# Graph network with two rounds of message passing: the matmuls of the rounds on four column strips of 32 in place of two of 64

## The reference

```python
h = jnp.maximum(_layernorm(x, axis=-1), 0.0)
for t in range(2):
    src = x[row]
    dest = x[col]
    m_input = jnp.concatenate([dest, src, edge_attr], axis=1)
    messages = m_input @ msg_W[t].T + msg_b[t]
    agg = jax.ops.segment_sum(messages, row, num_segments=x.shape[0])
    x = _gru_cell(agg, x, gru_Wih[t], gru_bih[t], gru_Whh[t], gru_bhh[t])
return x_in + x
```

## Time and profile before

| | |
|---|---|
| median of the runs | 2364.18 us (2 runs, 2361.75 to 2366.62) |
| span of the profiled execution | 2356.6 us |
| PE matmul busy | 1597.8 us (68%), 46870 records |
| PE weight loads busy | 1496.5 us (64%), 46870 records |
| DVE busy | 2175.2 us (92%) |
| ACT busy | 1953.9 us (83%) |
| POOL busy | 658.3 us (28%) |

### The profile page before, as it was taken

How to read it: one execution, slowest core, us unless ns; L and a number is a source line. 1 busy time by engine, 2 the same in 40 slices (tenths; PEclk the granted TensorE clock), 3 DMA queues, 4 the chain that set the end, 5 groups by cost and what they waited for, 6 DMA issues and landing times. The chain is left out here.

```text
span 2356.6 us, 126105 instructions
## 1 busy us (share of the span) xinstructions
PE 1597.8 (68%) x46870; PEld 1496.5 (64%) x46870; DVE 2175.2 (92%) x3629; ACT 1953.9 (83%) x4429; POOL 658.3 (28%) x853
## 2 busy tenths in 40 slices
PE   0000000000148899999999999959999999999996
PEld 0000000000138899999999999948899999999996
DVE  7999999999279899999999999958899999999996
ACT  4777895563248899999999999959899999999996
POOL 1000000000553444454544444511222222222222
PEclk9999999999959999999999999979999999999998
DMA  6100001211436666666677766647677777777773
GB/s 124 25 0 0 0 0 31 50 23 23 116 93 210 209 227 226 228 227 230 226 232 226 228 224 226 221 144 227 218 246 249 245 248 248 247 245 246 250 247 122
DMA packets 176134, 400.90 MB, mean 170 GB/s; under 512 B 73499, under 2 KB 77505, under 8 KB 175571
## 3 DMA queue, kind: packets, MB, share of 16 engines
q1 hardware_dynamic: 117047, 202.53, 27.1%
q0 software_dynamic: 57296, 195.19, 25.1%
q10 hardware_dynamic: 1708, 2.10, 0.3%
HBM read 384.73 MB, written 14.67 MB: 169 GB/s over the span
## 5 line engine op out<-in xcount | busy, mean ns | idle before, releaser
L1286 ACT ACTIVATE rows<-ps_rows 128x512 f16<-128x512 f32 x2744 | 1436.3, 647 | 47.2 <-PE ps_rows L1187 36.0
L1397 DVE TENSOR_TENSOR src<-iota_units,src_lane 128x2048 f16<-128x2048 f16 (+1 forms) x784 | 861.6, 1099 | 17.2 <-PE ps_sum L1205 13.7
L1207 PE MATMUL ps_sum<-rows,src 128*64 128x132 f16 x10976 | 585.6, 223 | 20.7 <-ACT rows L1286 14.0
L1187 PE MATMUL ps_rows<-rows_next,planes 128*64 128x128 f16 x10976 | 551.0, 220 | 32.9 <-DVE planes L1387 23.2
L1187 PE MATMUL ps_rows<-rows_now,planes 128*64 128x128 f16 x10976 | 559.8, 219 | 17.8 <-DVE planes L1387 7.8
L1205 PE MATMUL ps_sum<-src,rows 128*64 128x128 f16 x10976 | 563.9, 221 | 7.5 <-issue 6.4
L1387 DVE TENSOR_SCALAR planes<-planes,lane_no 128x2048 f16<-128x2048 f16 (+1 forms) x784 | 532.2, 679 | 5.6 <-DMA planes<-lanes_dram 5.3
L1187 PEld LDWEIGHTS ps_rows<-rows_now,planes 128*64 128x64 f16 x10976 | 425.2, 110 | 38.4 <-ACT rows L1286 14.4
L1187 PEld LDWEIGHTS ps_rows<-rows_next,planes 128*64 128x64 f16 x10976 | 412.3, 110 | 56.8 <-DVE planes L1387 23.9
L890 PE MATMUL ps_src<-ident,late 112*64 112x112 f32 x98 | 21.2, 394 | 607.3 <-DVE late L962 586.9
L1207 PEld LDWEIGHTS ps_sum<-rows,src 128*64 128x64 f16 x10976 | 404.8, 110 | 34.4 <-ACT rows L1286 21.5
(11 more groups left out here) (203 smaller groups left out, 2044.0 us busy)
## 6 DMA issues: line engine op xcount, KB each, us to landing
planes<-lanes_dram POOLq DMA_DIRECT2D x294, 512.0 KB, 4.8
planes<-lanes_dram SPq DMA_DIRECT2D x291, 512.0 KB, 4.6
planes<-lanes_dram POOLq DMA_DIRECT2D x98, 256.0 KB, 4.1
planes<-lanes_dram SPq DMA_DIRECT2D x97, 256.0 KB, 3.9
rows_now<-parts_dram SPq DMA_DIRECT2D x112, 32.0 KB, 1.7
rows_next<-parts_dram SPq DMA_DIRECT2D x112, 32.0 KB, 4.0
parts_dram<-rows_now SPq DMA_DIRECT2D x1, 3136.0 KB, 16.2
sorted_dram<-planes SPq DMA_DIRECT2D x1, 3136.0 KB, 11.6
```

The lines of the kernel that those rows point to most:

```text
L1187: last = nc.tensor.matmul(ps_rows[(u + NU * b) % 4][half * SLOTS:(half + 1) * SLOTS, k * 2 * H:(k + 1) * 2 * H], dst1[q][:, (c - q * QC) * ...
L1207: last = nc.tensor.matmul(ps_sum[b][at, 0:width], hot[:, at], row, start=(j == 0), stop=(j == J - 1))
L1286: nc.scalar.activation(rows[:, (u + NU * b) % ring, 0:n, 0:2 * H], cut(ps_rows[(u + NU * b) % 4][:])[:, 0:n, :], ACT.Copy).then_inc(rows_r ...
L1397: nc.vector.tensor_tensor(src1[q][:, 0:pairs_now], iota_units[:].rearrange("p (o l) k -> p o l k", o=1) .broadcast_to([P, pairs_now, P, 2] ...
```

## The change

All matmuls of the rounds now write 32 partitions in place of 64, and so use 32 columns of the array each; there are twice as many of them. The moving operands keep their width. The turns go through a helper, `turn_one`, that issues two matmuls where there was one. What is computed does not change, nor does anything on the other engines.

```diff
-HALVES = (slice(0, 64), slice(64, 128))
+STRIPS = tuple(slice(at, at + 32) for at in range(0, 128, 32))
...
-                            for half in range(2):
-                                c = 2 * j + half
+                            for at in STRIPS:
+                                c = 2 * j + at.start // SLOTS
                                 if c < C:
                                     last = nc.tensor.matmul(
-                                        ps_rows[(u + NU * b) % 4][half * SLOTS:(half + 1) * SLOTS, k * 2 * H:(k + 1) * 2 * H],
-                                        dst1[q][:, (c - q * QC) * SLOTS:(c - q * QC + 1) * SLOTS], rows_of[r % 2][:, c, :],
+                                        ps_rows[(u + NU * b) % 4][at, k * 2 * H:(k + 1) * 2 * H],
+                                        dst1[q][:, (2 * j - q * QC) * SLOTS + at.start:(2 * j - q * QC) * SLOTS + at.stop], rows_of[r % 2][:, c, :],
                                         start=True, stop=True)
...
-                            for at in HALVES:
+                            for at in STRIPS:
                                 if flipped:
...
+                        def turn_one(t, place, side):
+
+                            for at in STRIPS[:2]:
+                                last = nc.tensor.matmul(ps_T[place + at.start:place + at.stop, side:side + P], t[:, at], ident[:],
+                                                        start=True, stop=True)
+                            return last
...
-                        for at in HALVES:
+                        for at in STRIPS:
                             nc.tensor.matmul(ps_gates[at, to], turned_now[b][:, at], w_first[:, r, :], start=True, stop=False)
-                        for at in HALVES:
+                        for at in STRIPS:
                             last = nc.tensor.matmul(ps_gates[at, to], turned_now[b][:, P + at.start:P + at.stop], w_second[:, r, :],
                                                     start=False, stop=True)
```

More of the change, by code:

```diff
@@ L1215, in turn @@
                         wait(te, T_ready, k)
-                        low, high = HALVES
+                        def turn_one(t, place, side):
[3 more added lines that the diff above has]
+                            return last
                         if flipped:
                             te.wait_ge(extras_kept, 1)
-                            nc.tensor.matmul(ps_T[high, 0:P], copied[b][:], ident[:], start=True, stop=True)
-                            nc.tensor.matmul(ps_T[low, 0:P], scaled[b][:], ident[:], start=True, stop=True).then_inc(turned, 1)
+                            turn_one(copied[b], H, 0)
+                            turn_one(scaled[b], 0, 0).then_inc(turned, 1)
                             return
@@ L1223, in turn @@
                         te.wait_ge(joined_ready, k + 1)
[L1224 to L1227, removed]
+                        turn_one(joined[b], 0, 0)
+                        turn_one(copied[b], H, 0)
+                        turn_one(extras[b], H, P)
+                        turn_one(scaled[b], 0, P).then_inc(turned, 1)
                     def gates(k, b, half):
```

## The result

The changed kernel takes 4243.24 us (2 runs, 4232.01 to 4254.48) against 2364.18 us: a ratio of 1.793, with a 95% interval of 1.786 to 1.800. It is slower by 79%. The profiled execution is the run of 4232.01 us and has a span of 4230.4 us.

A forecast was written before the change was run, and what follows sets the result against it. PE was taken to set the pace, with instruction fetches deciding after the change: 2356.6 + 159 (first-time code) + 1716 (loops) = 4232 us of span, plus 8 us around it, 4240 us; range 2480 to 4750 us.

The forecast's parts named there:

- What bounds: Loops of both rounds: PE leads with ACT close behind; a faster PE gains nearly nothing, a slower one costs in full.
- The streams: PE's matmuls: four strips overlap as two halves do, 32 matmuls take the time of 16, gain and loss nil.
- The rival of a pace per matmul: Gathers and scatters: 28.4 ns for each matmul, +6.4 us a tile, about 3600 us; chance 0.13.
- First-time code: Written-out tiles and first loop iterations: 89 instruction packets at 4.0 us, 356 us in place of 197, +159 us.
- The loops: Other 43 iterations of each round: all code refetched, 9 × 4.0 = 36 us each, 3096 in place of 1380 us, +1716; chance 0.37.
- the bodies lie in eight or nine blocks: TensorE loop bodies of 1985 and 1955 instructions: 7.8 and 7.6 packets long, refetched each iteration if fewer than nine are held.
- packets come one at a time: Instruction queue in new code: one fetch follows another, each costing about 4.3 us.
- packets closer than 3.6 us: Instruction queue: packets nearer together than this would show the prediction wrong.
- The rival in which the loops stay: Loop bodies held in the engine, only first-time code slower: 2523 us, 2487 to 2576 with bounds; chance 0.25.
- that in which only some blocks fall out: Loops: two to four bare fetches an iteration in place of nine, about +9.5 us each, 3340 us; chance 0.15.
- fetches overlap once they are needed faster: Instruction fetch: one landing within 1.95 us of the last, stretches and loops cost nothing, 2357 to 2400 us; chance 0.07.
- The clock: PE's clock adds little: at 1.2 GHz 128 matmuls take 3.6 us, still under the fetch.

The follow-up runs named there:

- m_every_other: Changed kernel with only even tiles on four strips, odd tiles on two halves of 64, all work done: 2453.61 us, 1.036 of the kernel before.
- l1_shift: Changed kernel with one of four pairs left out of the scatter and 78 fulfilled waits ahead of TensorE's first round: 2505.24 us, 4210.22 us without the waits.
- a_long_body: Kernel before, still on two halves, with four tiles in the TensorE loop body in place of two: 2960.22 us, ratio 1.255.

## Why the prediction was right

The mechanism was right: the loop bodies no longer stay in the engine, and their fetches set the pace. That the time came out within 3 us is in good part luck, as the terms show.

**What bounds.** PE leads and a slower PE costs in full: right. ACT and DVE wait for PE in the profile after.

**The streams.** They were taken as nil, and they are: 0.45 us a unit in the changed kernel and 15.6 us an iteration in m_every_other. The rival of a pace per matmul, at 3600 us, falls with that.

**First-time code.** 89 packets at 4.0 us, 356 us. The queue has 42 + 43 in 182 + 189 us, so 85 packets in 371 us, 4.4 us each. The term was 15 us too small: I had taken less than the 4.3 us that the rows gave, and in these stretches the rows were right.

**The loops.** Nine packets of 4.0 us an iteration, 3096 us over 86 iterations. Measured: nine packets, 35.9 and 36.1 us an iteration, so 43 × 35.9 + 43 × 36.1 = 3096 us. That is luck. The fetches that follow each other are eight, 4.4 us apart as in first-time code, and the ninth adds only 0.8 to 1.1 us, since at the loop's end two are under way at once. I had one fetch in the row too many and each 0.4 us too short, and the two errors cancel. With the 4.3 us of the rows and nine in a row the term would have been 3328 us.

**Two steps were put wrongly.** I wrote that the bodies lie in eight or nine blocks and that the engine refetches when it holds fewer than nine. Both bodies lie in eight. The ninth packet fits the block behind the body, which would also be what pushes the first one out. The number of fetches was right and the reason for the ninth was not; l1_shift shows how much hangs on it. The other step is that packets come one at a time: I gave packets closer than 3.6 us as a sign of being wrong, and the pair at the loop's end is closer in every iteration. The step holds for straight code, where no two packets come closer than 3.0 us and the mean is 4.4 us. The rival in which the loops stay would have been right with a body one block shorter, and that in which only some blocks fall out is excluded by nine packets for eight blocks. That fetches overlap once they are needed faster is excluded by the 4.4 us; they overlap only where the loop goes back.

**The clock.** Said to add little, since execution stays below the fetch. The profile is in line with it: the mean clock in the loops is 0.84 and 0.86, and PE stands behind its blocks with "issue" as releaser. It was not tested by itself.

**The sum.** 4232 us of span forecast, 4230.4 us measured. Two small errors of opposite sign hide in it, first-time code too cheap by 15 us and all that lies outside these two terms too dear by some 16 us. The 8 us that the sum adds for what lies around the span are not there: the run of 4232.01 us has a span of 4230.4 us, 1.6 us less. The 8 us before are a difference between executions, and the two runs of the changed kernel differ by 22 us.

## What to carry to other kernels

Cutting matmuls into more and narrower ones is free in the array and not in the instruction stream. Count the instructions of TensorE's loop body, two for each matmul and four in fp32: if its blocks of 256 and the one behind them are more than eight, every iteration fetches all of its code, at some 4.4 us for each block of the body, and a shift of the code by some 80 instructions can be worth 1700 us, as here. And keep one width of the array over long stretches: each change of it cost 0.115 us.

## What the runs showed of the hardware

- Instruction blocks of 16 KB of straight code arrive one at a time, 4.4 us apart in the changed kernel, in its loops and in its first-time code, and 4.9 to 5.0 us in a_long_body. From the start of a packet until PE goes on it is 2.4 us in both, at 109 and at 163 GB/s.
- Where a loop that is not held goes back to its start, two blocks are fetched at once, 0.8 to 1.1 us apart in the mean.
- A loop on TensorE whose body lies in seven blocks is held (2505 us), the same body in eight is fetched anew each time (4210 us), with nine packets an iteration and not only those that did not fit.
- Four strips of 32 stream at once as well as two halves of 64: 32 matmuls of 128 columns in 0.45 us, 14 ns a matmul with its weight load. In the loop of the second round of m_every_other a tile on strips takes 7.8 us and one on halves 7.8 us.
- A change between widths 32 and 64, or 64 and 128, costs 0.115 us (0.34 us in place of 0.22 to 0.23).
